# q and k through DRAM one after the other, and x of the second attention turned by DMA, in a two-layer graph transformer kernel

## The reference

```python
# layer 0: attention over 4 relations, then a feed-forward net
q, k = heads(x @ Wq + bq), heads(x @ Wk + bk)              # 8 heads of 32
attn = softmax(q @ k.T / sqrt(32))
out  = sum over r of (attn * (adj == r)) @ heads(x @ Wv[r] + bv[r])
x = LN(x + out @ Wo + bo);  x = LN(x + gelu(x @ W1 + b1) @ W2 + b2)
# layer 1: attention over the edges
q, k, v = heads(x @ Wq), heads(x @ Wk), heads(x @ Wv)
e = leaky_relu(q @ k.T, 0.2)
h = softmax(where(adj > 0, e, -9e15)) @ v
out = LN(concat(LN(h), x) @ Wffn.T) + x
```

## Time and profile before

| | |
|---|---|
| median of 3 runs | 3144.58 us (3140.56 to 3147.18) |
| the profiled execution | 3143.89 us, span 3142.1 us |
| TensorE busy | 3016.0 us (96%) |
| VectorE busy | 2485.9 us (79%) |
| ScalarE busy | 2006.6 us (64%) |
| GpSimd busy | 1671.9 us (53%) |
| TensorE clock | 0.992 of full speed over the span |

### The profile page before, as it was taken

How to read it: one execution, slowest core, us unless ns; L and a number is a source line. 1 busy time by engine, 2 the same in 40 slices (tenths; PEclk the granted TensorE clock), 3 DMA queues, 4 the chain that set the end, 5 groups by cost and what they waited for, 6 DMA issues and landing times.

```text
span 3142.1 us, 75255 instructions
## 1 busy us (share of the span) xinstructions
PE 3016.0 (96%) x27909; PEld 2048.1 (65%) x27909; DVE 2485.9 (79%) x6763; ACT 2006.6 (64%) x3709; POOL 1671.9 (53%) x1512
## 2 busy tenths in 40 slices
PE   6999999999999989999999989999999999999994
PEld 3666666666666646666666666777777777777773
DVE  5888888888888865666666667888888888888882
ACT  4666666656666665666666646777777777777773
POOL 2555555545555544434344444666666666666664
PEclk9999999999999999999999999999999999999997
DMA  5445454444444432332323234444444445444440
GB/s 164 138 133 155 131 143 131 143 126 140 136 138 137 136 100 81 68 81 74 81 68 81 70 115 134 136 136 144 141 137 142 137 142 142 137 136 136 137 129 30
DMA packets 358336, 382.54 MB, mean 122 GB/s; under 512 B 99264, under 2 KB 266816, under 8 KB 357952
## 3 DMA queue, kind: packets, MB, share of 16 engines
q1 hardware_dynamic: 356800, 376.03, 41.5%
q10 hardware_dynamic: 1152, 1.52, 0.2%
HBM read 242.16 MB, written 118.49 MB: 115 GB/s over the span
## 4 chain that ended last, share of the span: by engine, by line
PE 65%; DVE 9%; issue 8%; POOL 7%; DMA 5%; ACT 3%; SPq 2%; DVEq 0%; POOLq 0%; ACTq 0%
PE bank_down L2287 4%; PE bank_score L1575 3%; PE bank_pairs L2166 3%; PE bank_down L2568 3%; PE bank_down L2567 3%; PE bank_down L2566 3%; PE bank_pairs L2566 3%; PE bank_pairs L2567 3%; PE bank_pairs L2568 3%; PE bank_score L2191 3%; PE bank_pairs L2169 3%; PE bank_pairs L2180 3%; PE bank_proj L2151 2%; PE bank_proj L2153 2%; PE bank_proj L2152 2%
## 5 line engine op out<-in xcount | busy, mean ns | idle before, releaser
L2516 DVE TENSOR_TENSOR f_gl<-f_act,f_gh 128x512 f16<-128x512 f32 x256 | 280.4, 1096 | 236.2 <-ACT f_act L2436 236.0
L1884 ACT ACTIVATE f_gh<-bank_pairs 128x512 f32<-128x512 f32 x512 | 304.1, 594 | 252.3 <-PE bank_pairs L2169 252.1
L2095 DVE CUSTOM_DVE_ANT_0 b_junk<-bank_score,b_mask 128x256 bf16<-128x256 f32 x1024 | 390.3, 419 | 40.4 <-issue 39.9
L1408 DVE TENSOR_TENSOR a_linked<-a_prob,a_mask 128x1024 f32<-128x1024 f32 x256 | 358.8, 1402 | 0.6 <-ACT a_prob L1204 0.6
L1987 POOL TENSOR_TENSOR f_xb<-f_gh 128x512 f32<-128x512 f32 x256 | 335.4, 1310 | 34.8 <-ACT f_gh L1884 34.5
L2431 ACT ACTIVATE f_gh<-bank_pairs,s_f_b 128x512 f16<-128x512 f32 x256 | 175.4, 685 | 244.3 <-PE bank_pairs L2568 244.3
L1971 POOL TENSOR_TENSOR b_nw_root<-b_nw_var,b_minus_halves 128x2 f32<-128x2 f32 x128 | 112.4, 878 | 409.8 <-DVE b_nw_neg_mean L2036 409.8
L1204 ACT ACTIVATE a_prob<-bank_down 128x1024 f32<-128x1024 f32 x256 | 258.9, 1011 | 106.4 <-PE bank_down L1489 100.8
L1401 DVE TENSOR_REDUCE a_neg_max<-bank_pairs 128x4 f32<-128x1024 f32 x256 | 307.4, 1201 | 4.6 <-PE bank_pairs L1502 4.4
L1890 ACT ACTIVATE bank_pairs<-bank_pairs 128x512 f32<-128x512 f32 x512 | 305.7, 597 | 0.0
L2566 PE MATMUL bank_down<-s_w,f_gh 128*128 128x256 f16 x1024 | 279.1, 273 | 2.2 <-ACT a_prob L1204 1.4
(11 more groups left out here) (279 smaller groups left out, 9394.1 us busy)
## 6 DMA issues: line engine op xcount, KB each, us to landing
qk_scratch<-a_qk SPq DMA_DIRECT2D x64, 512.0 KB, 2.9
qk_scratch<-b_qk SPq DMA_DIRECT2D x64, 512.0 KB, 2.9
a_stack_a<-qk_scratch SPq DMA_DIRECT2D x192, 128.0 KB, 3.0
a_stack_b<-qk_scratch SPq DMA_DIRECT2D x192, 128.0 KB, 3.0
first_rows<-qk_scratch SPq DMA_DIRECT2D x192, 128.0 KB, 3.0
f_gl<-qk_scratch SPq DMA_DIRECT2D x192, 128.0 KB, 3.0
a_x_sb<-x_t SPq DMA_DIRECT2D x64, 256.0 KB, 3.5
a_adj_sb<-adj_t SPq DMA_DIRECT2D x64, 256.0 KB, 3.1
```

Of the source, the lines that this page charges most:

```text
L1408: nc.vector.tensor_tensor(linked[:, k], prob[:, k], mask[:, be[1] % 2].unsqueeze(1).to_broadcast([P, 2, NT * N]), ALU.mult).then_inc(link_ ...
L1884: nc.scalar.activation(prob[:, he], score_t[s].rearrange("p t n -> p (t n)"), ACT.Exp, scale=ALPHA).then_inc(exp_done, 1)
L2095: last = nc.vector.tensor_tensor_reduce(junk[:, s, it], score[s][:, it], mask[:, i, it], -1.0, 3e38, ALU.add, ALU.min, neg_max[:, i, col:c ...
L2516: nc.vector.tensor_tensor(gl[:, bu[1] % 2, f], act32[:, f % 2], gh[:, bu[1] % 2, f], ALU.subtract).then_inc(low_done, 1)
```

## The change

Both attentions: q's parts and k's parts are stored with two DMAs, k's with a semaphore of its own (`k_stored`). SP issues q's store, waits for k's low part, issues k's store, and loads q's three pieces when q is stored and k's three when k is.

Second attention: the fp32 turn on TensorE is gone. x is loaded four slots earlier, ScalarE (slot 6) and VectorE (slot 7) cut it into halves in a new tile `x_nodes`, node-major in SBUF, and SP turns each half by a DMA transpose (`turn_x`, slot 7) into `xh` and `xl`, for which q waits (`x_turned`). The other edits give semaphores that the stages share to new uses, and change no instruction.

```diff
                     if bp := due(t, h, "store_qk"):
...
-                        sp.wait_ge(qk_low, parts_made)
+                        sp.wait_ge(qk_low, parts_made + 1)
                         if exists(back(bp, 2)):
                             sp.wait_ge(stack_loaded[back(bp, 2)[1] % RING], scratch_read)
-                        sp.dma_start(scr[i].rearrange("k p n -> p k n"), qk[:, i]).then_inc(qk_stored[i], 16)
+                        sp.dma_start(scr[i, 0:2].rearrange("k p n -> p k n"), qk[:, i, 0:2]).then_inc(qk_stored[i], 16)
+                        sp.wait_ge(qk_low, parts_made + 2)
+                        sp.dma_start(scr[i, 2:4].rearrange("k p n -> p k n"), qk[:, i, 2:4]).then_inc(k_stored[i], 16)
                         sp.wait_ge(qk_stored[i], parts_stored)
                         if stacks_read is not None:
                             sp.wait_ge(scores_t_done, stacks_read)
-                        for blk, (kq, kk) in enumerate(((0, 2), (1, 2), (0, 3))):
-                            for which, kind in ((0, kq), (1, kk)):
+                        for which, kinds in ((0, (0, 1, 0)), (1, (2, 2, 3))):
+                            if which:
+                                sp.wait_ge(k_stored[i], parts_stored)
+                            for blk, kind in enumerate(kinds):
                                 sp.dma_start(stack[r4][DH * blk:DH * (blk + 1), which],
...
-    AT = {"load": 4, "load_adj": 4, "xT": 8, "xh": 8, "xl": 9, "q": 10, "q_hi": 10, "q_lo": 11, "linked": 7, "k": 12, "k_hi": 12, "k_lo": 13,
+    AT = {"load": 0, "load_adj": 4, "xh": 6, "xl": 7, "turn_x": 7, "q": 10, "q_hi": 10, "q_lo": 11, "linked": 7, "k": 12, "k_hi": 12, "k_lo": 13,
...
+                    if bx := due(t, h, "turn_x"):
+                        i, r = bx[1] % 2, bx[1]
...
+                        sp.wait_ge(xh_ready, past["xh_ready"] + count(bx, 1, 1))
+                        sp.dma_start_transpose(xh[r].rearrange("p c n -> p (c n)").rearrange("p (g n) -> p g n", n=P),
+                                               x_nodes[:, i, 0].rearrange("p c t n -> p (c t n)")).then_inc(x_turned[i], 16)
+                        sp.wait_ge(xl_ready, past["xl_ready"] + count(bx, 1, 1))
+                        sp.dma_start_transpose(xl[r].rearrange("p c n -> p (c n)").rearrange("p (g n) -> p g n", n=P),
+                                               x_nodes[:, i, 1].rearrange("p c t n -> p (c t n)")).then_inc(x_turned[i], 16)
...
-                        sp.wait_ge(qk_low, past["qk_low"] + parts_made)
                         sp.wait_ge(q_zeroed, rows_zeroed)
...
                     if bx := due(t, h, "xh"):
-                        act.wait_ge(proj_done, past["proj_done"] + count(bx, 4, 1))
...
-                        nc.scalar.activation(xh[bx[1]], proj[:],
-                                             ACT.Copy).then_inc(xh_ready, 1)
+                        i = bx[1] % 2
+                        act.wait_ge(x_loaded[i], past["x_loaded"] + uses(bx, XS) * 16)
+                        if exists(back(bx, 2)):
+                            act.wait_ge(x_turned[i], uses(back(bx, 2), 2) * 32)
+                        nc.scalar.activation(x_nodes[:, i, 0].rearrange("p c t n -> p t c n"),
+                                             x_sb[:, i].rearrange("p t (c n) -> p t c n", c=DC), ACT.Copy).then_inc(xh_ready, 1)
...
                     if bx := due(t, h, "xl"):
-                        r = bx[1]
+                        i = bx[1] % 2
                         dve.wait_ge(xh_ready, past["xh_ready"] + count(bx, 1, 1))
-                        nc.vector.tensor_tensor(xl[r], proj[:].rearrange("p (c n) -> p c n", c=DC), xh[r], ALU.subtract).then_inc(xl_ready, 1)
+                        nc.vector.tensor_tensor(x_nodes[:, i, 1].rearrange("p c t n -> p t c n"),
+                                                x_sb[:, i].rearrange("p t (c n) -> p t c n", c=DC),
+                                                x_nodes[:, i, 0].rearrange("p c t n -> p t c n"), ALU.subtract).then_inc(xl_ready, 1)
...
-                    if bx := due(t, h, "xT"):
-                        pe.wait_ge(x_loaded[bx[1] % XS], past["x_loaded"] + uses(bx, XS) * 16)
...
-                        for c in range(DC):
-                            for tt in range(NT):
-                                last = nc.tensor.transpose(proj[:, c * N + tt * P:c * N + (tt + 1) * P],
-                                                           x_sb[:, bx[1] % XS, tt, c * P:(c + 1) * P], ident[:])
-                        last.then_inc(proj_done, 1)
...
                             if j == 0:
-                                pe.wait_ge(xl_ready, past["xl_ready"] + count(bp, 1, 1))
+                                pe.wait_ge(x_turned[bp[1] % 2], uses(bp, 2) * 32)
```

More of the change, by code:

```diff
@@ L1059, in attention_first @@
         qk_stored = [sem(f"qk_stored{i}") for i in range(2)]
+        k_stored = [sem(f"k_stored{i}") for i in range(2)]
         stack_loaded = [sem(f"stack_loaded{i}") for i in range(RING)]
@@ L1147, in slot @@
                         i, r4 = bp[1] % 2, bp[1] % RING
-                        parts_made = held(count(bp, 2, 2))
+                        parts_made = count(bp, 2, 0)
                         scratch_read = held(uses(back(bp, 2), RING) * LOADS)
@@ L1213, in slot @@
                                 act.wait_ge(qk_stored[i], uses(back(bp, 2), 2) * 16)
+                                act.wait_ge(k_stored[i], uses(back(bp, 2), 2) * 16)
                             for c in range(DC):
@@ L1750, in attention_second @@
         proj_done = again("proj_done")
+        x_turned = [sem(f"x_turned{i}") for i in range(2)]
         xh_ready = again("xh_ready")
@@ L1775, in attention_second @@
         sums_done = sem("sums_done")
-        sums_out = sem("sums_out")
-        heads_out = sem("heads_out")
-        sums_turned = sem("sums_turned")
+        sums_out = again("sums_out")
+        heads_out = again("heads_out")
+        sums_turned = again("sums_turned")
         rinv_ready = sem("rinv_ready")
@@ L1810, in slot @@
                         i = bx[1] % XS
-                        if (n := after(back(bx, XS), 4, 1)) is not None:
-                            sp.wait_ge(proj_done, past["proj_done"] + n)
+                        if (n := after(back(bx, XS), 1, 1)) is not None:
+                            sp.wait_ge(xh_ready, past["xh_ready"] + n)
+                            sp.wait_ge(xl_ready, past["xl_ready"] + n)
                         sp.dma_start(x_sb[:, i], rows(x_in, bx)).then_inc(x_loaded[i], 16)
+                    if bx := due(t, h, "turn_x"):
+                        i, r = bx[1] % 2, bx[1]
+                        if number(bx) == EARLY:
+                            wait_old(sp, "up_done")
+                        if (n := after(back(bx, XB), 1, 1)) is not None:
+                            sp.wait_ge(out_done, n)
+                        sp.wait_ge(xh_ready, past["xh_ready"] + count(bx, 1, 1))
[4 more added lines that the diff above has]
+                                               x_nodes[:, i, 1].rearrange("p c t n -> p (c t n)")).then_inc(x_turned[i], 16)
                     if ba := due(t, h, "load_adj"):
@@ L1829, in slot @@
                         i, r4 = bp[1] % 2, bp[1] % RING
+                        rows_zeroed = held(count(bp, 1, 1))
                         parts_made = held(count(bp, 2, 2))
-                        rows_zeroed = held(count(bp, 1, 1))
                         scratch_read = held(uses(back(bp, 2), RING) * LOADS)
@@ L1845, in slot @@
                             sp.wait_ge(stack_set, 2)
-                        for blk, (kq, kk) in enumerate(((0, 2), (1, 2), (0, 3))):
-                            for which, kind in ((0, kq), (1, kk)):
+                        for which, kinds in ((0, (0, 1, 0)), (1, (2, 2, 3))):
+                            if which:
+                                sp.wait_ge(k_stored[i], past["k_stored"] + parts_stored)
+                            for blk, kind in enumerate(kinds):
                                 sp.dma_start(stack[r4][DH * blk:DH * (blk + 1), which],
@@ L2193, in slot @@
                         last.then_inc(scores_done, 1)
-                    if bx := due(t, h, "xT"):
-                        pe.wait_ge(x_loaded[bx[1] % XS], past["x_loaded"] + uses(bx, XS) * 16)
-                        if number(bx) == 0:
-                            wait_old(pe, "row_out")
-                        if (n := after(back(bx, 1), 1, 1)) is not None:
-                            pe.wait_ge(v_ready, past["v_ready"] + n)
-                        for c in range(DC):
-                            for tt in range(NT):
-                                last = nc.tensor.transpose(proj[:, c * N + tt * P:c * N + (tt + 1) * P],
-                                                           x_sb[:, bx[1] % XS, tt, c * P:(c + 1) * P], ident[:])
-                        last.then_inc(proj_done, 1)
```

(6 more changed lines are left out.)

43 lines of the change are left out of this document (23 added, 20 removed).

## The result

The changed kernel takes 3132.05 us (median of 7 runs, 3128.34 to 3135.09) against 3142.99 us (7 runs of the kernel before, 3140.42 to 3147.18): ratio 0.9966, 95% interval 0.9955 to 0.9977. I had forecast 3154 us, slower. The time lies in the range given, but the direction is wrong.

What follows compares the result with a forecast made beforehand. The prediction took TensorE, streaming at 19.06 us per graph in the second attention, as the bound, VectorE nearly critical. +22 (VectorE's chain), -5 and -6.5 (stack waits) and 0 made +10.5, taken as 10, on 3143.89: 3154 us, range 3130 to 3178.

Steps and rivals of the forecast that it cites:

- What bounds the kernel: Steady second attention: TensorE streams at 19.06 us per graph; VectorE's chain ending in f_y has 0.10 us slack.
- (1): Second attention: four fp32 turns of x per graph leave TensorE, 0.44 us; by TensorE alone the period would be 18.62.
- (2): Second attention, ScalarE: the cast xh moves between b_hh and v_out, inside a 1.37 us idle gap; cost 0.
- (3): Second attention, VectorE: xl moves from behind f_y to directly behind b_hl, into the chain to f_y, for 0.6 us.
- (4): Second attention: xl, now reading only SBUF, contends with GpSimd; f_y slips 0.5 us (0.35 to 0.61), giving +22 us.
- Rival B: Second attention: xl fills VectorE's waiting for GpSimd without holding it; about 3127 us; faster if insertion below 0.1; chance 0.13.
- my own -5 and -6.5: Forecast gains in us: vanishing stack waits in the steady second attention, and earlier stacks from separate q and k.
- (5): Steady second attention: TensorE's waits for stacks of q and k, about 5 us, vanish: -5 us.
- (6): Second attention, SP: two DMA transposes per graph land before q starts, with some 2 us left; cost 0.
- (7): First attention: separate q and k bring the last stack 1.5 to 2 us earlier; -6.5 us, bounds -2 and -9.
- (8): Start of second attention: shorter stack waits against transposes queued behind loads and a store; 0, bounds -3 and +4.

## Why the prediction was wrong, step by step

- **What bounds the kernel**: right. TensorE streamed, VectorE's chain had next to no slack; shown by the early mask with the half sum behind f_y, which give nothing with the turn on TensorE (3129.09 against 3129.32 us) and 27 us without it (3105.39 against 3132.05).
- **(1), (2), (3)**: right. The turn of x was worth 0.44 us, the chain took it all, TensorE stands at L2264's place, and xh cost nothing: ScalarE's idling of 1.37 us is 0.85 in the changed kernel, and no steady wait of TensorE ends with it.
- **(4) is the step that failed**: "linked and mask are bound to these two and slip with them, by 0.5, and so does f_y". The order of the turns was as I said. GpSimd was held by 0.37 us, and mask slipped by it. But f_y slipped by 0.10. I followed the slip through linked and mask and took the rest of the chain as rigid. It is not. neg_some waits for GpSimd too, for a half sum with a gap of 0.32 us in front of it; the gap swallowed the slip, and only 0.18 us came back, because the late mask now held that half sum. And f_y had been released by TensorE, not by offset, which took another 0.10. I forecast 19.46 us for the period; it is 19.09. This is 0.37 us times 56, or 21 us, and turns the sum from +10.5 to about -10. Rival B came nearest to the time (3127), though its reason was another: it had GpSimd not held at all. It had also set the point from which "faster" holds too low: at its 0.1 us the period is as before, but my own -5 and -6.5 make the kernel faster all the same, and that is what was measured.
- **(5)**: right in kind. The stack waits vanish. They were worth more than 5 us: before, the mean distance of the turns was 19.20 at a median of 19.06, 7.8 us in 56 graphs; in the changed kernel it is 19.10 at 19.09.
- **(6)**: right. A transpose takes 1.20 or 1.26 us to issue and lands 3.1 or 2.5 us after its start (medians), 4.7 at most, and one wait of 0.4 us for it, before the steady part, is all that TensorE shows.
- **(7)**: -6.5 foreseen, -4.5 in these two executions, inside the bounds. From the first to the last maximum the ten kernels with the split took 1100.3 to 1103.2 us, the four without it 1105.8 to 1109.5; the means differ by 5.8, so the forecast was good. Of the waits for stacks the 7.3 us of the first 80 became 2.9; the 4.1 of the steady part are gone, but 2.8 of them came back as waits for a_hl (16.6 to 19.4), where I had allowed 1.4.
- **(8)**: 0 foreseen, -2 measured, inside the bounds, and it is the split's: the stretch to the first turn of the offsets took 23.8 to 24.2 us in the four kernels without it and 21.1 to 21.8 in nine of the ten with it (26.4 with xl twice). The turn alone, without the split, cost some 5 us behind it. The end of the program, 1.5 us longer, differs as much between other kernels.

## What to carry to other kernels

When an instruction is inserted into a chain, follow the delay through to the last member, and ask of each one what ended its wait: a wait for a third engine may have a gap in front of it that swallows the delay, and one that runs late anyway may have been released by the engine that the change relieves. A gain on the bounding engine shows only if the next chain has slack; here moving one mask and making one half sum wait turned 0.3% into 1.1%. Before a run is taken as the control for a chain, see in its trace that the chain's end moved: the early mask in the kernel before left it where it was. Look at small instructions with long rows (16 columns in 0.60 us): they show who is waited for, and a wait deliberately placed on the engine with time to spare can be the cheapest cure.

## What the runs showed of the hardware that I had not expected

- How short a VectorE instruction is does not protect it from GpSimd: neg_some and offset, 128x16, took 0.17 us with GpSimd idle and 0.43 to 0.78 and up to 1.19 beside it. The maxima and f_y, which read PSUM with one SBUF tile, took 0.41 to 0.42 and 0.68 to 0.69 in all kernels.
- The price of a meeting depends on who comes first: the same xl of 0.68 us cost GpSimd 0.34 to 0.37 when it began 0.2 us ahead, and lost 1.08 itself when it began 0.4 us behind. What the graph pays is another thing: 1.42 us in the kernel with xl twice, nothing in the graph at 2520 us, where mask then met no half sum.
- Two stretches differed between executions of kernels with the same code in them, by 2.5 us and more (to the first maximum, 26.6 to 29.1 without the split) and by 5.9 (the feed-forward stage, 707.6 to 713.5). A difference of two spans holds this too.
